# Time loop of a recurrent layer on one Trainium2 core: outer product, sum, tanh and joint product in two halves of 64 columns

## The reference, cut to what matters

```python
def step(S, inp):
    logits_t, k_t, v_t, beta_t, q_t = inp
    ...  # uw: weights of the two blocks chosen, kn: the key over its length
    retrieved = jnp.einsum('bnij,bnj->bni', S, kn)
    delta = v_t - retrieved
    outer = delta[..., :, None] * kn[..., None, :]
    S_upd = jnp.tanh(beta_t[..., None] * S + outer)
    w = uw[..., None, None]
    S_new = (1.0 - w) * S + w * S_upd
    Sq = jnp.einsum('bnij,bj->bni', S_new, q_t)
    ...
```

## Time and profile before

| what | value |
|---|---|
| time, median of 3 runs | 8015.45 us (8005.39 to 8021.79) |
| the profiled execution | 8023.4 us, its span 8021.6 us |
| instructions | 237061 |
| busy share of the span | PE 83%, PEld 49%, DVE 75%, ACT 36%, POOL 46% |
| mean granted clock of TensorE | 0.931 |

### The profile page before, as it was taken

One profiled execution on the slowest core, in us unless ns is written; L12 is line 12 of the kernel. 1 busy time (PEld: TensorE's weight loads), 2 busy tenths in 40 slices (PEclk: granted clock), 3 DMA queues, 4 the chain that ended last, 5 costly groups with the idle time before them and its releaser, 6 DMA issues. The chain is left out here.

```text
span 8021.6 us, 237061 instructions
## 1 busy us (share of the span) xinstructions
PE 6678.4 (83%) x89269; PEld 3954.0 (49%) x89449; DVE 6026.7 (75%) x12205; ACT 2874.5 (36%) x5767; POOL 3689.6 (46%) x4646
## 2 busy tenths in 40 slices
PE   4888888888875655787876999999999999999997
PEld 2666666666631222252443554555555455555543
DVE  7777777777767668786874877777777777777776
ACT  2111111111134232313223555455554555555554
POOL 0333333333300000110302777777777777777774
PEclk7999999999987877988987999999999999999999
DMA  0000000000000000000003222222222222222222
GB/s 21 1 1 0 1 1 0 1 0 1 0 6 1 1 14 0 0 1 0 1 1 113 74 70 71 71 70 79 68 74 73 71 71 73 71 71 74 68 71 73
DMA packets 213313, 292.27 MB, mean 36 GB/s; under 512 B 27872, under 2 KB 193280, under 8 KB 206592
## 3 DMA queue, kind: packets, MB, share of 16 engines
q1 hardware_dynamic: 212224, 277.76, 11.6%
HBM read 235.94 MB, written 13.66 MB: 31 GB/s over the span
## 5 line engine op out<-in xcount | busy, mean ns | idle before, releaser
L2917 POOL TENSOR_TENSOR big<-big 128x512 f32<-128x512 f32 x776 | 1076.3, 1413 | 68.8 <-DMA big<-norms 57.6
L836 POOL TENSOR_TENSOR big<-big 128x128 f32<-128x128 f32 x1024 | 415.2, 405 | 1275.1 <-DVE big L782 1274.8
L2272 PE MATMUL banks<-hidden,big 128*128 128x256 f32 x3104 | 800.2, 402 | 120.1 <-DVE big L2741 49.7
L600 ACT ACTIVATE banks<-banks 128x128 f32<-128x128 f32 x1024 | 268.3, 262 | 1759.0 <-DVE banks L763 1759.0
L1956 POOL TENSOR_TENSOR big<-big 128x448 f32<-128x448 f32 (+10 forms) x160 | 142.5, 891 | 1618.7 <-DVE weights_odd L1820 1546.8
L2334 PE MATMUL banks<-big,hidden 128*32 128x512 f32 x6144 | 791.8, 611 | 0.0
L489 PE MATMUL banks<-big 128*128 128x256 f32 x2050 | 727.3, 437 | 60.8 <-ACT big L574 59.4
L2272 PEld LDWEIGHTS banks<-hidden,big 128*128 128x128 f32 x3104 | 580.4, 196 | 383.9 <-DVE big L2741 141.4
L2313 PE MATMUL banks<-big 32*32 32x64 f32 (+1 forms) x49152 | 599.6, 224 | 199.3 <-issue 199.0
L2313 PEld LDWEIGHTS banks<-big 32*32 32x32 f32 x49152 | 517.7, 104 | 437.2 <-issue 436.5
L334 PE MATMUL banks<-big,weights_even 128*128 128x512 f32 (+5 forms) x1056 | 499.5, 668 | 249.2 <-DVE big L1088 45.1
(11 more groups left out here) (360 smaller groups left out, 14046.4 us busy)
## 6 DMA issues: line engine op xcount, KB each, us to landing
big<-norms SPq DMA_DIRECT2D x776, 128.0 KB, 3.0
big<-qk SPq DMA_DIRECT2D x50, 512.0 KB, 4.6
big<-vo SPq DMA_DIRECT2D x25, 1024.0 KB, 5.7
small<-tables SPq DMA_DIRECT2D x196, 128.0 KB, 2.3
weights_odd<-ffn SPq DMA_DIRECT2D x25, 537.5 KB, 5.8
big<-tables SPq DMA_DIRECT2D x98, 128.0 KB, 2.2
weights_even<-tables SPq DMA_DIRECT2D x98, 128.0 KB, 2.9
hidden<-big SPq DMA_DIRECT2D x171, 64.0 KB, 2.4
```

Of the source, the lines that this page charges most:

```text
L836: nc.gpsimd.tensor_tensor(full(u["kS"][s % 2]), full(S), by(u["ko_c"]), ALU.mult).then_inc(*e.did(("kS", s)))
L2272: mm = self.nc.tensor.matmul(bank[:, n * QTOK:(n + 1) * QTOK], u["w" + name.lower()][:, (2 * g + n) * P:(2 * g + n + 1) * P], u["xs"][:, a ...
L2917: self.nc.gpsimd.tensor_tensor(x, x, u["norms"][:, n, g].unsqueeze(1).broadcast_to([P, 2, QTOK]), ALU.mult).then_inc(*e.did(("scaled", f, ...
```

## The change

`outer`, `arg` and `T` become two tiles each of 64 columns, that is two blocks of the four. The two halves of `outer` lie side by side in bank 2. The halves of `arg` and `T` lie in banks 3 and 6, one bank for each half. VectorE issues both halves of the outer product, then both halves of the sum, each waiting for its half of the outer product; ScalarE takes tanh of each half as its sum is done; VectorE multiplies each half of `T` with both weights as it is done, into the same `kwT`. TensorE and the new state wait for the second half of the joint product, and L489 for the second half of the outer product. The rest of the step stays as it is.

```diff
-        step_bank=core.bank[0:2], outer=core.bank[2][:, 0:128],
-        arg=core.bank[3][:, 0:128], T=core.bank[3][:, 128:256], out_bank=[core.bank[4], core.bank[7]],
+        step_bank=core.bank[0:2], outer=[core.bank[2][:, 0:64], core.bank[2][:, 64:128]],
+        arg=[core.bank[3][:, 0:64], core.bank[6][:, 0:64]], T=[core.bank[3][:, 128:192], core.bank[6][:, 128:192]], out_bank=[core.bank[4], core.bank[7]],
...
-            pe.wait_ge(*e.after("outer", before, **back))
+            pe.wait_ge(*e.after("outer", before, 1, **back))
...
-            act.wait_ge(*e.after("arg", s))
-            nc.scalar.activation(u["T"], u["arg"], ACT.Tanh).then_inc(*e.did(("T", s)))
+            act.wait_ge(*e.after("arg", s, 0))
+            nc.scalar.activation(u["T"][0], u["arg"][0], ACT.Tanh).then_inc(*e.did(("T", s, 0)))
+            act.wait_ge(*e.after("arg", s, 1))
+            nc.scalar.activation(u["T"][1], u["arg"][1], ACT.Tanh).then_inc(*e.did(("T", s, 1)))
...
-            tt(cut(u["outer"]), cut(u["step_bank"][s % 2][:, 0:P]), spread(u["kn_c"], s), ALU.mult).then_inc(
-                *e.did(("outer", s)))
-            dve.wait_ge(*e.after("outer", s))
-            tt(u["arg"], u["outer"], u["bS"], ALU.add).then_inc(*e.did(("arg", s)))
+            for c in range(2):
+                tt(cut(u["outer"][c]), cut(u["step_bank"][s % 2][:, columns(c)]), spread(u["kn_c"], s, c),
+                   ALU.mult).then_inc(*e.did(("outer", s, c)))
+            for c in range(2):
+                dve.wait_ge(*e.after("outer", s, c))
+                tt(u["arg"][c], u["outer"][c], u["bS"][:, columns(c)], ALU.add).then_inc(*e.did(("arg", s, c)))
...
-            dve.wait_ge(*e.after("T", s))
-            tt(u["kwT"].rearrange("p (k n i) -> p k n i", k=2, n=BLK),
-               cut(u["T"]).unsqueeze(1).broadcast_to([P, 2, BLK, NST]),
-               u["both_c"][:, :, :, s].unsqueeze(3).broadcast_to([P, 2, BLK, NST]), ALU.mult).then_inc(*e.did(("kT", s)))
+            for c in range(2):
+                dve.wait_ge(*e.after("T", s, c))
+                tt(kwT[:, :, blocks(c), :], cut(u["T"][c]).unsqueeze(1).broadcast_to([P, 2, HB, NST]),
+                   u["both_c"][:, :, blocks(c), s].unsqueeze(3).broadcast_to([P, 2, HB, NST]), ALU.mult).then_inc(*e.did())
+            e.name_last("kT", s)
             e.name_last("wT", s)
```

More of the change, by code:

```diff
@@ L745, in cells_vector, with spread @@
     chain()
-    def spread(v, s):
-        return v[:, :, s].unsqueeze(2).broadcast_to([P, BLK, NST])
-    cut = lambda a: a.rearrange("p (n i) -> p n i", n=BLK)
+    HB = BLK // 2
+    blocks = lambda c: slice(c * HB, (c + 1) * HB)
+    columns = lambda c: slice(c * HB * NST, (c + 1) * HB * NST)
+    def spread(v, s, c):
+        return v[:, blocks(c), s].unsqueeze(2).broadcast_to([P, HB, NST])
+    cut = lambda a: a.rearrange("p (n i) -> p n i", n=HB)
+    kwT = u["kwT"].rearrange("p (k n i) -> p k n i", k=2, n=BLK)
     with e.turns("time", CELL_TURNS):
```

## The result

| what | before | after |
|---|---|---|
| time, median of 4 runs | 8011.95 us (8005.39 to 8021.79) | 7919.48 us (7915.02 to 7931.43) |
| ratio | | 0.9883, 95% interval 0.9867 to 0.9899 |
| the profiled execution, its span | 8023.4, 8021.6 us | 7921.0, 7919.1 us |
| first to last outer product (1023 steps) | 2072.6 us | 1968.0 us |
| a usual step | 1.963 us | 1.846 us |

The kernel is 92.5 us faster (7912 had been forecast). In a second comparison, on another occasion, the changed kernel stood at 0.9876 (0.9859 to 0.9892) of the kernel before.

What follows compares the result with a forecast made beforehand. No engine was full; a closed dependent chain bound the first layer's loop, VectorE and ScalarE idling in turn. 8023.4 - 111 (992 x 0.112) + 8 = 7920 us profiled, median 7912; range 7885 to 7970, about 0.80.

Steps and rivals of the forecast that it cites:

- late steps: First layer's time loop: VectorE's longer text makes code arrive late, costing 8 us more, from 3 to 31.
- steps that TensorE ends: Some 32 loop steps where the outer product came late behind TensorE's L508; no gain counted in them.
- the row with another operand, L1876: Three-operand 64-element VectorE instruction, 0.272 us: upper bound for a 64-column one; its 0.19 us spacing was the other end.
- The copies' row: Two 64-element PSUM copies (L1872) occupying 0.35 us: the next independent VectorE instruction starts 0.136 us behind.
- Rival 2: VectorE halves reading and writing one PSUM bank do not overlap, standing 0.230 us apart: about 8120 us; chance 0.09.
- rival 3: Loop step: overlap holds, but halves cost more or leave the queue late; gain 0.037 to 0.08, 7945 to 7987 us; chance 0.14.
- Rival 1: VectorE halves reported in batches: first sum waits for the second outer half; 8038 us; chance 0.04.
- The tail: Behind the joint product, new state and L508 wait for both halves, so 0.58 us a step stays.

Runs made afterwards that it cites:

- The first experiment: Changed kernel with each half of the sum issued right behind its own outer half, instead of behind both; 8134.2 us, usual step 2.046 us.

## Why the prediction was right

The sum, term by term, from starts in the trace (medians), in us behind the step's first outer half:

| step of the sum | predicted | measured |
|---|---|---|
| second outer half | 0.136 | 0.142 |
| sums | 0.272, 0.408 | 0.273, 0.409 |
| tanh | 0.535, 0.671 | 0.534, 0.665 |
| joint halves | 0.774, 0.984 | 0.775, 0.983 |
| end of the second joint half | 1.271 | 1.264 |
| gain of a step | 0.112 | 0.117 |
| lost to late steps, and to steps that TensorE ends | 8 + 32 x 0.112 = 12 | 15 |

**The sizes.** A 64-column instruction took 228 and 225 ns (0.230 from the difference of two widths), half a joint product 287 (287), tanh of 64 columns 208 (206). Widening or narrowing the instruction next to it by a slope from this trace was good to 5 ns, and the row with another operand, L1876, was rightly an outer bound.

**The distance of two free instructions** was the term on which the sign hung. The copies' row gave 0.136; the outer halves, which read and write PSUM and write one bank, stand 0.142 apart. The Trainium skill's price from PSUM (VectorE: DVE Perf Modes, section on the TRN2 errata), which the prediction turned into an estimate of 0.19 us, does not hold here as the distance of two such instructions. Rival 2 (no overlap in PSUM, 0.19 to 0.23) falls by the same number, and rival 3 (a smaller gain) by the sizes.

**Rival 1**, that the first sum waits for the second outer half, would have put it at 0.399; it stood at 0.273. The first experiment shows the case in which results really are awaited in turn: a loss of 0.083 us a step.

**The tail** stayed at 0.58 us, since both of its paths wait for the whole joint product; the three kernels that split it show that they are of one length within about 0.025 us.

**Late steps** were priced at 8 us more; counted by steps they cost 12. The cause that the prediction gave, code arriving late, was an inference from one late instruction. The distances of 6.4 to 10.7 steps tie such instructions to blocks of 128, so more code does bring more of them, but that code was still on its way is not borne out: each time the transfer begins only after the late instruction. So the price came near without its mechanism. Steps that TensorE ends were priced at the gain forgone, 4: the first four steps of the turns cost 4 more, and the waits for TensorE, which the profile counts, 6 more.

**The total.** The sum gave 7920 us for the profiled execution, which took 7921.0. That it met so closely is in part luck: 5 us more of gain in the usual steps stand against 3 us more of losses and 2 us outside the loop. The median forecast, 7912, lies 7.5 us under the measured one because it took the median to stand 8 us under the profiled execution, as before the change; after it stood 1.5 under.

## What to carry to other kernels

Where one element-wise chain runs back and forth between two engines, split it along its free columns and issue the same operation of both halves before the next operation: a result awaited at once cost 0.26 us here at 64 columns, an independent instruction 0.14. Split every operation up to the point where the results meet, since a split further up is worth something only if the next one passes the lead on, and leave alone what has a second path of the same length beside it. Count the instructions of a written-out loop, waits too: the code itself costs time at its block ends and at the jump back.

## What the runs showed of the hardware that I had not expected

- Late instructions recur every 128 instructions of VectorE's queue in the loop, computed waits counted, by up to 0.33 us each, once a block. A transfer of 8192 bytes on q14 begins 0.67 us after each (the median), and none runs while it waits.
- TensorE's loop of 23 instructions a step goes back to its start without a transfer on q8; with 28 a step 9 transfers appear in each turn and the next turn's first product came after 2.85 us of "issue" (time in which the engine waited for nothing that the profile shows). With 25 a step, and without L525, 3 or 6 transfers are left and the turn's end is as with 23.
- Without L525, some 0.2 us of TensorE time a step, and without one wait, the granted clock in the loop fell from 0.96 to 0.70, and the kernel took 8212 to 8399 us instead of 7949.5, though the usual steps at full clock were no longer than with it.
